# One-hot products of a gathered group: 128 moving columns against the columns that the group's position can span

## The reference

```
x = x + gnn(layernorm(x), edge_index, edge_weight, ...)
x = x + ffn(layernorm(x)[None], ...)[0]

def hconv(x, src, dst, ew, w1, b1, w2, b2, g, b):
    h = relu(x @ w1 + b1)
    msg = ew[:, None] * h[src]
    agg = segment_sum(msg, dst, num_segments=N)
    h = agg @ w2 + b2
    return relu(bn(h, g, b))
```

## Time and profile before

| | us |
|---|---|
| median of 3 runs | 4848.33 |
| lowest, highest | 4831.88, 4853.95 |
| span of the profiled execution | 5228.2 |
| first layer's aggregate | about 179 to 1750 of the span |
| second layer's aggregate | about 1866 to 3412 of the span |
| experts | 3412 to the end |

### The profile page before, as it was taken

The page is one execution under the profiler, slowest core; times in us unless marked ns, Lnnn a source line. Parts: engine busy times, 40 slices in busy tenths (PEclk is TensorE's granted clock), DMA queues, the critical chain, the costliest instruction groups (busy, mean ns, idle before and its releaser), DMA issues. The chain is left out here.

```text
span 5228.2 us, 71544 instructions
## 1 busy us (share of the span) xinstructions
PE 4623.3 (88%) x25508; PEld 3800.6 (73%) x25508; DVE 2688.7 (51%) x6606; ACT 2435.6 (47%) x4218; POOL 2110.6 (40%) x2284
## 2 busy tenths in 40 slices
PE   6778888888999579888988988649999999999999
PEld 5667777666677467776666666548888888888888
DVE  7666666566333464522222222366666666666665
ACT  4655556666211263300000000057777777777777
POOL 1466666566666456666666666630000000000000
PEclk9889999999999789999999999779999999999999
DMA  5467777566755247876666666431111111001110
GB/s 155 148 210 271 243 240 245 188 211 217 236 198 201 77 141 268 277 243 218 218 219 205 226 212 224 131 96 25 30 28 33 33 33 33 24 26 33 33 28 15
DMA packets 546618, 770.23 MB, mean 147 GB/s; under 512 B 149720, under 2 KB 441411, under 8 KB 546262
## 3 DMA queue, kind: packets, MB, share of 16 engines
q1 hardware_dynamic: 328176, 382.01, 21.7%
q0 software_dynamic: 100944, 273.96, 16.4%
q10 hardware_dynamic: 117142, 109.65, 6.5%
HBM read 605.58 MB, written 147.26 MB: 144 GB/s over the span
## 5 line engine op out<-in xcount | busy, mean ns | idle before, releaser
L1106 PE MATMUL pf<-work 128*128 128x330 f32 (+4 forms) x3528 | 1251.9, 491 | 63.3 <-DMA work<-front 31.3
L1054 POOL DMA_INDIRECT wst<-h,src_col x1040 | 1000.3, 962 | 541.9 <-issue 275.0
L1106 PEld LDWEIGHTS pf<-work 128*128 128x128 f32 x3528 | 661.0, 197 | 402.2 <-issue 220.1
L2096 DVE TENSOR_TENSOR f_hl<-f_hf,f_hh 128x1024 fp32r<-128x1024 f32 (+1 forms) x400 | 479.7, 1199 | 636.3 <-ACT f_hf L1959 636.0
L1952 ACT ACTIVATE f_hh<-f_p,f_sh,f_sc 128x512 fp32r<-128x512 f32 (+1 forms) x800 | 571.7, 768 | 395.9 <-PE f_p L2194 394.5
L1273 ACT ACTIVATE ah<-agg 128x1024 fp32r<-128x1024 f32 (+1 forms) x50 | 51.8, 1037 | 1464.2 <-DVE agg L1420 1086.6
L1138 PEld LDWEIGHTS ps<-oh,wst 128*128 128x128 f32 x4160 | 543.4, 203 | 144.5 <-issue 99.6
L1138 PE MATMUL ps<-oh,wst 128*128 128x128 f32 x4160 | 560.7, 288 | 88.6 <-issue 55.1
L1054 POOL DMA_INDIRECT f_xr<-h,src_col x518 | 497.7, 961 | 282.8 <-issue 134.0
L1054 POOL DMA_INDIRECT f_u<-h,src_col x512 | 491.1, 959 | 260.5 <-issue 136.7
L1959 ACT ACTIVATE f_hf<-f_p,f_sh,f_sc 128x512 f32<-128x512 f32 (+1 forms) x800 | 572.5, 775 | 0.0
(11 more groups left out here) (285 smaller groups left out, 7648.0 us busy)
## 6 DMA issues: line engine op xcount, KB each, us to landing
work<-h SPq DMA_DIRECT2D x216, 512.0 KB
work<-front SPq DMA_DIRECT2D x50, 924.0 KB
front<-agg ACTq DMA_DIRECT2D x12, 3300.0 KB
work<-front SPq DMA_DIRECT2D x50, 756.0 KB
work<-front SPq DMA_DIRECT2D x50, 660.0 KB
work<-front SPq DMA_DIRECT2D x50, 580.0 KB
front<-agg ACTq DMA_DIRECT2D x8, 2600.0 KB
work<-front SPq DMA_DIRECT2D x25, 832.0 KB
```

The source lines that it names most:

```text
L1054: g.indirect_dma_start(G[t % R], None, h_dram[layer], bass.IndirectOffsetOnAxis(ap=src_col[:, col:col + 1], axis=0)).then_inc(ga[t % R], 16)
L1106: ins = g.matmul(pF[:, k, 0:count * w].rearrange("p (s c) -> p s c", c=w), HB[a % 2][0:r, n, k * P:(k + 1) * P], x, start=b == 0, stop=b = ...
L2096: g.tensor_tensor(hlo[l][q % 2][:, :, 0:nn], hf[l][:, :, 0:nn], hhi[l][q % 2][:, :, 0:nn].bitcast(fp32), ALU.subtract).then_inc(f_lo[l], 1)
```

## The change

The product reads and writes `width` columns in place of 128. The planner's price for a group's 16 instructions changes with it, from 111 ns each to `max(64, 8 + width * 5 / 6)`.

```
-            other = [16 * 111 + sum(max(224, NB * hot(layer, t)[4] * 9 // 10) for t in hot_behind(layer, q))
+            other = [16 * max(64, 8 + width(FGL[layer] + q) * 5 // 6) + sum(max(224, NB * hot(layer, t)[4] * 9 // 10) for t in hot_behind(layer, q))
                      + (560 if q > ZERO_Q[layer] else 0) for q in range(NQL[layer])]
...
+                            wide = width(FGL[layer] + q)
                             for k in range(KC):
                                 for t in tiles_of[q]:
                                     if k == 0:
                                         g.wait_ge(ga[t % R], gathered_value(layer, t))
-                                    ins = g.matmul(pS[bank_of[q]][:, k, :], G[t % R][:, k * P:(k + 1) * P], OH[t % RO],
+                                    ins = g.matmul(pS[bank_of[q]][:, k, 0:wide], G[t % R][:, k * P:(k + 1) * P], OH[t % RO][:, 0:wide],
                                                    start=t == tiles_of[q][0], stop=t == tiles_of[q][-1])
                             ins.then_inc(g_mm, 1)
```

## The result

The change makes the kernel slower by 0.66%: 4878.85 us (median of 5 runs, 4870.15 to 4893.16) against 4851.69 us (5 runs), ratio 1.0066, 95% interval 1.0048 to 1.0084. The forecast was 4898 us.

A forecast was written before the change was run, and what follows sets the result against it. The prediction took PE as the busiest engine in the aggregates, with POOL and DMA sharing the delay. Pace 0, latency -5, plan 0, clock +55 gave +50 us on the 4848 us median: 4898 us, range 4825 to 5005.

The forecast's parts named there:

- Bounds: In the two aggregates PE is the busiest engine, 86% and 87%; POOL's gathers need 2600 of their 3117 us.
- Pace, 0 us: Group product in the aggregates: 8284 pairs stay at 112 ns, set by loading 128 weight columns; 0 us saved.
- one-column row: L702, a float32 product moving one column with 128 weight columns, also takes 112 ns a pair, so narrowing saves nothing.
- transpose at 70 ns: L2172 moves 40 columns at 70 ns with a shorter weight load; at its pace 348 us of PE's work would go.
- the pace falls: Rival: the aggregates' product pairs go at 70 ns, half of 348 us comes through, 4673 us; chance 0.12.
- Latency, -5 us: Each group's last matmul in the aggregates ends up to 30 ns sooner; 5 us saved, ends 0 and 16.
- Plan, 0 us with 10 to either side: Planner's new price moves 279 of 882 units by one or two groups; total work the same, 0 us.
- Clock, +55 us: Narrower products in the aggregates lengthen low-clock time by half: 88 us of PE's work, 55 us coming through.
- the case: Rival, slower by the clock: the aggregates lose the full clock more often, +5 to +170 us, 4853 to 5018; chance 0.50.
- The signs: Changed profile: sixteen instructions about 1.9 us, weight loads 186 to 192 ns, aggregates' clock 0.90 to 0.92, experts 1816 us.
- nothing moved: Rival: weight loads set the pace and the aggregates' clock stays at 0.94 and 0.93; 4843 us, chance 0.35.
- more than 348 us: PE work the change would save by the skill page's gap rule alone; the prediction set it aside for the one-column row.

The follow-up runs named there:

- filler runs: One unread 256-column matmul added per group, planner's old price: with narrow product 4976.20 us, ratio 1.0272; with the 128-column product of the kernel before 4959.75 us, 1.0233.
- second trace: The kernel before, unedited, run and profiled once more: 4846.61 us, span 4844.8 us.
- earlier trace: First profile of the kernel before, no edit, from which the prediction argued: span 5228.2 us.
- streams of 56 columns: Separate kernel, not the reference's computation: 600 weight-load and matmul pairs per stream, at five widths; at 56 columns 128.25 us after rest, 67.10 us from full clock.
- product alone: Kernel before with only the product narrowed, planner's old price kept: 4884.13 us against 4847.01, ratio 1.0075.
- 64 columns at least: Kernel before with the product narrowed to width but never under 64 columns, planner's old price: 5265.25 us against 5249.8, ratio 1.0034.

## Why the prediction was right, point by point

**Bounds.** I read PE as the engine that mattered, POOL as a near second. The filler runs say that PE's work counts by about 0.5; the prediction had let 55 of 88 us through, 0.62. In the second trace PE is busy for 92% and 95% of the aggregates, not for 86% and 87% as in the earlier trace rows, and POOL issues nearly without a break in layer 1. The trace that I argued from had waits that the timed runs lacked; the span 7.8% above the median was the sign, and putting the sum to the median unscaled was a guess. The windows of the earlier trace rows are also cut a little off: the products of layer 0 run to 1796.5 us, and those of layer 1 begin at 1935.1.

**Pace, 0 us.** Right, and the step that decided that nothing is won. The one-column row was the nearest row, and the transpose at 70 ns was not. The rival "the pace falls" is refuted by the streams of 56 columns. Only the first interval of a group has become shorter in the changed kernel (48 ns at 56 columns in the group at 2409 us, 109 ns before at 2401 us; the other fourteen are 111 to 112 ns in both).

**Latency, -5 us.** Not seen. 16 pairs end 0.04 to 0.06 us sooner, but no run isolates what that is worth; it is within what the measurement can tell.

**Plan, 0 us with 10 to either side.** Right: +5 us by itself. Together with the narrow product it may even help (27 us for both against 37 us for the product alone); this stays open, as the two weren't timed together, and on which chip the change ran isn't known.

**Clock, +55 us.** The mechanism is right, and it was a bet: no row tied the clock to the width, as the prediction says, and it gave the case a chance of 0.50. I let the time at the lower level grow by half, from 405 to 608 us. In the traces near the medians it more than doubled, but from less: 161 to 338 us, 177 more in place of 203. Base and growth were both wrong and nearly cancelled; that the increase came out close is luck. And I took 55 / 203 = 0.27 us for each microsecond of it; it was 0.19. Part of that gap is the share that comes through, 0.5 by the filler runs in place of 0.62 (203 us at 0.5 x 0.87 x 0.51 would be 45 us); the rest isn't accounted for. 177 x 0.19 = 34 us in the traces, 27 us in the medians. That is the term that was mis-sized: the sum said +50.

**The signs.** Of those that the prediction named for the profile, one failed. It put the mean clock of the aggregates at 0.90 to 0.92 if the clock's step was right, and at 0.94 and 0.93 if nothing moved; it is 0.94 and 0.94, which by that test alone reads as "nothing moved". The test was built on the trace of 5228 us. Against the right trace, with 0.96 and 0.98, the fall is there. The other signs came: sixteen instructions in 1.9 us, weight loads of 186 to 192 ns at the full clock, PEld busier, the experts at 1816 us. PE's busy time was to fall with the shorter ends and rose by 56 us.

I had also written that the fall follows gaps in PE's work and that narrow products make such stretches worse. That is only half of it. Of the 68 us from 174 us on, the last 44 have hardly a gap (PE busy for 43.0 of 44.5 us). The clock had fallen ahead of them, while PE waited at the change of stages, in both kernels; with the narrow product it stayed low. The run that is narrow in the first 60 groups alone has the same stretch of 68 us, and the one that is wide in them has not. The separate streams show the same without gaps at all.

The Trainium skill ("TensorE: Matmul & The Clock Gate", section Back-to-back issue gap) gives an isolated gap that shrinks with the columns; here it did not, from 128 down to 1 column, with a weight load to every matmul. The prediction's "more than 348 us" by that rule needs the measured 112 ns scaled by the same proportion; the formula as it stands gives 72 / 2.4 = 30 ns a pair, 249 us (an estimate from the page's figure). The same page's advice to keep PE continuously busy to get out of the low clock holds for 128 and 96 columns here; streams of 56 and fewer were continuously busy by the profile for 128 us and did not get out.

## What to carry to other kernels

Where each matmul brings its own weights of 128 columns, a float32 product had its moving columns up to 128 for nothing in these runs; look for the narrowest product of the same kind in the trace before you cut them. And look at the granted clock of the stretch: a narrow product leaves the engine's time as it was and can cost it the clock, which every other matmul of the stage pays for (the hot products at 200 us: 1.49 us in place of 0.87). What a lost microsecond of PE is worth has to be asked of the stage: here about half came through. POOL's gathers, which fill 97% of layer 1, are the likely taker of the rest; no run isolates that.

## What the runs showed of the hardware that I had not expected

- The clock of a stream depended on the level at which it began: 600 pairs of 56 columns ran at 0.50 throughout after a rest and at 1.00 throughout after a stream of 512 columns (128.25 and 67.10 us for the same instructions).
- A stream with PE and PEld both busy all the time can lose the full clock: 28 columns from full took 123.63 us at 0.52.
- The same kernel took 4847 us on one chip and 5250 us on another. The traces at hand place the difference in the two stages with indirect gathers: they take 2707 us in the second trace, 3093 us in that of the earlier trace rows and 3111 us in that of "64 columns at least", which ran on the slower chip, while the experts take 1820, 1816 and 1815 us. What on the slower chip holds the gathers up is open.
